# Attention step of a fused transformer layer: two quads' sums in one bank region, projections in even steps and transposes in odd ones

## The chip, the cores and the metric

The kernel runs on one core of a Trainium2 chip. The metric is the device time of the whole kernel in microseconds (us). Engines: PE (TensorE, with PEld for its weight loads), DVE (VectorE), ACT (ScalarE), POOL (GpSimd), SP (SyncE, which issues most DMAs).

## What is computed

Sixteen sequences of 256 tokens with 128 features. The input is normalised (no gain), goes through causal attention with 16 heads of 8 features, and beside it through a mixture of eight expert networks (one shared, seven routed, two of these for each token). The results are added to the input.

```
xn = layernorm(x)
q, k, v = xn @ in_proj.T            # 16 heads of 8, q / sqrt(8)
att = softmax(q @ k.T + causal mask) @ v @ out_proj.T
w = top 2 of softmax(xn @ wr.T + rb), made to sum to 1
ffn = expert(xn; shared) + sum_e w[e] * expert(xn; e)   # expert: (silu(x g) * (x u)) d
out = x + att + ffn
```

## The kernel before

Each engine runs its own list of instructions in order, written out by hand; semaphores (`wait_ge`, `then_inc`) tie the lists together. There are three parts.

*The front*: rounds f = 0 to 15, one for each sequence ("batch"): normalise, transpose the tokens, split them into a high and a low part, values and routing logits. Between some rounds `FRONT` places the first attention steps, with negative numbers. `idle` are matmuls without use that fill PE's pauses (L1023).

*The attention loop*: 64 steps n, `quad(n)` = (batch b, quad j of four heads). A step works on several quads at once. PE's `step(n)` (L984): first scores (`scores(n, 0)`: for the row maxima of quad n+3 and, transposed, for the exponentials of quad n), the transposes of the sums of quad n-2 (L996), the sums of quad n-1 (`sums`, L976 and L979: exponentials times values, into columns 256 to 511 of bank J), second scores, a side job (`side`: query projection at j = 0, key projection at j = 1 for batch b+3, transposes of the scaled sums of batch b-1 at j = 3, two counts for the routing) into columns 256 to 511 of bank X, and `maxima(n+2)` into columns 0 to 255 of J.

ACT's `step(n)` (L690): exponential of one pair of heads (L702), `unscaled(n-2)` (L688: sums out of bank X), exponential of the other pair, the copy for the side job (L711 the high part of a projection, L720 the turned sums), sums from J to `ot` (L732), `queries(n+2)` (L679), and at j = 0 the batch's values into zero-padded columns (L740). POOL's step: a causal select behind each exponential (L616), up to step 22 splitting expert weights (`split_block`), and in steps 23 to 62 altogether 64 indirect DMAs (`send`, L592), between and behind the selects: one in 16 of the 40 steps, two in 24. DVE's `step(n)` (L1334): first row maximum (L1345), a piece of the routing (steps in `N_ROUTE`), second row maximum, the low part of a projection (L1379), the negated maxima (L1358 to L1361), and at j = 2 `scaled(b-1)`: reciprocal (L1325) and multiply (L1329). SP's step loads heads' queries and keys (L485), and stores a batch's projections at j = 2 (L475).

The loop around an exponential: both pairs of heads use the same two banks for their transposed scores, so the second scores of a step wait for the first exponential, and the next step's first scores for the second. Two engines never use one bank at the same time, which is what many of the waits are for (`bank_read`).

*The experts*: `NT * MT` units u of gate, up and down products. Steps 64, 65 and 66 of attention lie in its units 0, 2 and 4.

The printed functions are those that the diff touches.

## Time and profile before

| what | value |
|---|---|
| median of 3 runs | 467.76 us (467.54 to 468.66) |
| profiled execution | 465.75 us, its span 464.0 us |
| PE busy | 431.9 us (93%) |
| DVE busy | 360.9 us (78%) |
| ACT busy | 315.1 us (68%) |
| POOL busy | 295.4 us (64%) |

The profile is one execution. "Busy" is the time in which an engine had an instruction under way; matmuls are pipelined and their ends are modelled. "[x <-E L]" behind an instruction says that its engine was idle for x us ahead of it and what ended that. "issue" is a wait that the profile has no releaser for. In views by time, neighbouring instructions of a kind are one row with their number ("x2"). TensorE's granted clock was full throughout.

### The profile page before, as it was taken

The page shows a single profiled execution, that of the slowest core. Times are in us where ns is not written, and L with a number is a line of the kernel's source. Part 1 is how long each engine was busy: PE and PEld are TensorE (multiplying, and loading weights), DVE is VectorE, ACT ScalarE, POOL GpSimd, SP SyncE. Part 2 cuts the span into 40 slices and gives each one's busy share as a digit, 9 for nine tenths or more (in the row PEclk, how much of TensorE's full clock was granted, in tenths as well). Part 3 has the DMA queues.
Part 4 walks back from the last instruction along what each step waited for, and adds up shares of the span by engine and source line. Part 5 has one row for each costly group of instructions (what it writes and reads, how often), then busy time and mean ns, then how long its engine had stood idle before and what let it go on. Part 6 is the DMA issues. An engine that isn't in the chain of part 4 may idle for free.

```text
span 464.0 us, 12501 instructions
## 1 busy us (share of the span) xinstructions
PE 431.9 (93%) x3983; PEld 323.9 (70%) x3987; DVE 360.9 (78%) x802; ACT 315.1 (68%) x709; POOL 295.4 (64%) x423
## 2 busy tenths in 40 slices
PE   8888898989899999999888999999999999999995
PEld 3766556656666666666666577888888888887783
DVE  5885999999878887877777077777777777776986
ACT  2756777767677777777676866666767776666552
POOL 1425888788888888888888900447457588775200
PEclk9999999999999999999999999999999999999999
DMA  8777799999875666655549226768868867822762
GB/s 232 225 226 256 199 378 292 296 325 353 283 247 159 172 188 173 184 161 153 154 114 335 69 59 181 255 195 279 288 210 279 282 209 258 270 92 68 254 182 70
DMA packets 60415, 99.84 MB, mean 215 GB/s; under 512 B 11045, under 2 KB 29226, under 8 KB 59328
## 3 DMA queue, kind: packets, MB, share of 16 engines
q1 hardware_dynamic: 55872, 90.57, 62.1%
q0 software_dynamic: 4480, 8.47, 5.5%
q8 instruction: 34, 0.56, 0.5%
q14 instruction: 29, 0.24, 0.2%
HBM read 60.85 MB, written 38.94 MB: 215 GB/s over the span
## 4 chain that ended last, share of the span: by engine, by line
PE 62%; DVE 13%; POOL 5%; ACT 4%; issue 3%; SPq 2%; DMA 1%; DVEq 0%; POOLq 0%; ACTq 0%
PE ps L846 12%; PE ps L847 12%; PE ps L848 12%; DVE sb_blockmax L1345 7%; PE ps L915 5%; PE ps L976 5%; PE ps L923 4%; ACT sb_work L702 3%; POOL xs L592 3%; PE ps L1145 3%; POOL sb_work L616 2%; PE ps L996 2%; PE ps L1134 2%; PE ps L979 2%; SPq L475 1%
## 5 line engine op out<-in xcount | busy, mean ns | idle before, releaser
L1345 DVE TENSOR_REDUCE sb_blockmax<-ps 128x6 f32<-128x768 f32 x128 | 121.5, 956 | 30.1 <-PE ps L923 24.4
L702 ACT ACTIVATE sb_work<-ps 128x768 f32<-128x768 f32 x128 | 104.4, 815 | 55.5 <-PE ps L911 54.2
L644 POOL DMA_INDIRECT ys<-sb_v_all,sb_xn_all x76 | 80.0, 1053 | 64.0 <-DVE sb_v_all L1466 46.4
L616 POOL TENSOR_SCALAR_AFFINE_SELECT sb_work<-sb_work 128x512 f32<-128x512 f32 x128 | 82.5, 646 | 24.9 <-ACT sb_work L702 23.2
L847 PE MATMUL ps<-sb_ring,sb_wb 128*128 128x512 f32 (+5 forms) x231 | 83.1, 360 | 0.0
L592 POOL DMA_INDIRECT xs<-sb_xn_all,sb_posu x64 | 62.8, 981 | 10.7 <-issue 10.7
L1444 DVE TENSOR_TENSOR sb_v_all<-ps,sb_v_all 128x512 f32<-128x512 f32 (+3 forms) x93 | 57.3, 616 | 14.1 <-ACT sb_v_all L793 9.9
L915 PE MATMUL ps<-sb_ring 32*128 32x256 f32 x256 | 49.2, 374 | 13.0 <-ACT sb_work L702 7.2
L793 ACT ACTIVATE sb_v_all<-ps 128x512 f32<-128x512 f32 (+3 forms) x93 | 49.8, 535 | 6.2 <-PE ps L848 5.4
L915 PEld LDWEIGHTS ps<-sb_ring 32*128 32x128 f32 x256 | 25.4, 181 | 36.6 <-issue 33.1
L846 PE MATMUL ps<-sb_ring,sb_wb 128*128 128x512 f32 (+1 forms) x138 | 50.8, 368 | 0.0
L923 PE MATMUL ps<-sb_mask_b,sb_ident_b 128*128 128x256 bf16 x256 | 50.2, 278 | 0.0
L907 PE MATMUL ps<-sb_ring 32*128 32x256 f32 x256 | 49.2, 381 | 0.4 <-ACT sb_work L702 0.3
L848 PE MATMUL ps<-sb_ring,sb_wb 128*128 128x512 f32 (+1 forms) x138 | 48.9, 355 | 0.0
L847 PEld LDWEIGHTS ps<-sb_ring,sb_wb 128*128 128x128 f32 (+2 forms) x231 | 42.5, 184 | 6.1
L976 PE MATMUL ps<-sb_work 128*32 128x256 f32 x512 | 40.9, 390 | 4.2 <-issue 1.6
L801 ACT ACTIVATE sb_qk_l<-sb_v_all 128x512 fp32r<-128x512 f32 (+3 forms) x46 | 26.7, 581 | 26.5 <-DVE sb_v_all L1444 20.7
L801 ACT ACTIVATE sb_qk_h<-sb_v_all 128x512 fp32r<-128x512 f32 (+3 forms) x47 | 26.9, 573 | 25.3 <-DVE sb_v_all L1444 19.2
L1452 DVE TENSOR_TENSOR sb_ring<-sb_v_all,sb_qk_h 128x512 fp32r<-128x512 f32 (+3 forms) x47 | 29.8, 633 | 15.8 <-ACT sb_qk_h L801 15.4
L1452 DVE TENSOR_TENSOR sb_ring<-sb_v_all,sb_qk_l 128x512 fp32r<-128x512 f32 (+3 forms) x46 | 29.3, 637 | 12.6 <-ACT sb_qk_l L801 11.7
L586 POOL TENSOR_TENSOR sb_wb<-sb_o_all,sb_wb 128x128 fp32r<-128x128 f32 (+1 forms) x72 | 30.9, 456 | 2.0
L919 PE MATMUL ps<-sb_ring 32*128 32x128 f32 x256 | 30.1, 217 | 0.0
(165 smaller groups left out, 1071.3 us busy)
## 6 DMA issues: line engine op xcount, KB each, us to landing
sb_wb<-wd SPq DMA_DIRECT2D x50, 384.0 KB, 4.3
sb_ring<-qk SPq DMA_DIRECT2D x64, 256.0 KB, 3.4
wd<-sb_wb SPq DMA_DIRECT2D x8, 1088.0 KB, 6.0
sb_wb<-wd SPq DMA_DIRECT2D x25, 320.0 KB, 3.4
xs<-sb_o_all SPq DMA_DIRECT2D x19, 260.0 KB, 3.7
qk<-sb_ring SPq DMA_DIRECT2D x32, 128.0 KB
sb_work<-ys SPq DMA_DIRECT2D x16, 256.0 KB, 3.3
sb_xn_all<-xs SPq DMA_DIRECT2D x15, 260.0 KB, 3.6
```

The source lines that it names most:

```text
L592: pool.indirect_dma_start(out=xs_d, out_offset=bass.IndirectOffsetOnAxis(ap=posu[:, k, t:t + 1], axis=0), in_=xn_all[:, t, :], in_offset=N ...
L616: pool.affine_select(out=o, in_=o, compare_op=ALU.is_ge, fill=0.0, base=0, pattern=[[0, 4], [1, 128]], channel_multiplier=-1)\
L644: pool.indirect_dma_start(out=ys_d, out_offset=bass.IndirectOffsetOnAxis(ap=row, axis=0), in_=yst[i % NYS][:, EMB * j:EMB * j + EMB], in_o ...
L702: act.activation(part.rearrange("p (k h q) -> p h k q", h=2, q=128), ps[:, 4:6, 0:HEAD].rearrange("p h (k q) -> p h k q", q=128), ACT.Exp, ...
L846: pe.matmul(out, wh, xh_, start=start, stop=False, skip_group_check=True)
L847: pe.matmul(out, wh, xl_, start=False, stop=False, skip_group_check=True)
L848: return pe.matmul(out, wl, xh_, start=False, stop=stop, skip_group_check=True)
L915: return pe.matmul(S[h][:, 0:256], q, k, start=True, stop=False, skip_group_check=True)
L923: return pe.matmul(out, ident_b[:, :], mask_b[:, :].unsqueeze(1).to_broadcast([128, 2, 128]), start=False, stop=True, skip_group_check=True)
L976: pe.matmul(J[32 * h:32 * h + 32, 256:512], v_sb[b % 2][:, 0, 4 * j + h, :], p[:, h // 2, h % 2, 1:3, :], start=True, stop=False, skip_gro ...
L1345: dve.tensor_reduce(blockmax[:, a:b + 1, 0:3], ps[:, a:b + 1, 0:HEAD].rearrange("p h (k c) -> p h k c", c=128), AX.X, ALU.max).then_inc(s[ ...
L1452: dve.tensor_tensor(hl[u % 2][0:n, 0:z], hf[u % 2][0:n, 0:z], hh[u % 2][0:n, 0:z].bitcast(F32), ALU.subtract).then_inc(s["hl"], 1)
```

## The change

The values of odd quads are laid 16 columns further right in their 32 zero-padded columns than those of even quads. The sums of an odd quad are added to those of the even one before it, in the same region of bank J (`start` is set for even quads only, and `maxima` sets it for even m only from m = 2 on). So one copy to `ot`, one pair of transposes and one copy out of bank X, now with 144 columns instead of 72, serve two quads.

PE's transposes of sums move from between first scores and sums to the end of odd steps (`across`), together with the turned sums of batch b-2 (at j = 1) and the counts; the projections stand in even steps (`project`: keys of batch b+3 at j = 0, queries of batch b+4 at j = 2). ACT does the copies out of bank X between the two exponentials of the following step (`between`) and copies a batch's values in two halves in odd steps (`batch_values`). DVE does the low part of a projection one step after PE's projection, between the two row maxima and ahead of the routing (`projection_low`), and the multiply of `scaled` in two halves. The front begins at step -14; the keys of batch 2 move from round 7 to round 5, the queries of batch 3 from step 0 to round 9, and the idle matmuls of rounds 10, 12 and 13 wait for `lq` 4. Out of the diff here: counts, buffers' views and waits that only change their numbers.

```diff
 
 
...
+        STEPS = range(-14, NQ + 3)
+
+        FRONT = {0: range(-14, -10), 2: range(-10, -6), 5: [-6, -5, -4], 7: [-3], 9: [-2], 11: [-1]}
         SENDS = TOPK * TILES
 
...
         def isb(b):
             return 0 <= b < NB
 
+        def projected(n):
+
+
+            b, j = quad(n)
+            x = b + 4 if j == 2 else b + 3
+            return (x, j == 0) if j in (0, 2) and isb(x) else None
+
+        def pair_out(n):
+
+            return (n - 3) // 2 if n % 2 and 0 <= (n - 3) // 2 < NQ // 2 else None
+
         def turned(n):
 
 
             b, j = quad(n)
-            return b - 1 if j == 3 and isb(b - 1) and isb(b) else NB - 1 if n == NQ + 2 else None
+            return b - 2 if j == 1 and isb(b - 2) else NB - 1 if n == NQ + 2 else None
 
         def side_out(n):
 
...
+            def unscaled(p):
...
+                c, half = divmod(p, 2)
+                act.wait_ge(s["T"], p + 1)
+                if half == 0 and c >= 2:
                     act.wait_ge(s["nm"], c - 1)
-                view = X[:, 0:256].rearrange("p (t h c) -> p t h c", t=2, c=32)
-                act.activation(xo[c % 2][:, :, j, :, :], view[:, :, :, 0:HD + 1], ACT.Copy).then_inc(s["xc"], 1)
+                view = X[:, 0:256].rearrange("p (t k x) -> p t k x", t=2, k=8)
+                act.activation(xo[c % 2][:, :, half, :, :, :].rearrange("p t h e c -> p t (h e) c"),
+                               view[:, :, :, 0:HD + 1], ACT.Copy)\
+                    .then_inc(s["xc"], 1)
...
+            def projection_high(n):
+
+                x, keys = projected(n)
+                act.wait_ge(s["pk" if keys else "pq"], x + 1)
+                if isb(x - 2):
+                    act.wait_ge(s_qd[(x - 2) % 2], stored(x - 2))
+                at = 256 if keys else 0
+                act.activation(qk_h[x % 2][:, at:at + 256], side_out(n), ACT.Copy)\
+                    .then_inc(s["hk" if keys else "hq"], 1)
...
+            def between(n):
+
+
+                if n % 2:
+                    if projected(n - 1) is not None:
+                        projection_high(n - 1)
+                    return
+                if pair_out(n - 1) is not None:
+                    unscaled(pair_out(n - 1))
+                if turned(n - 1) is not None:
+                    turned_out(turned(n - 1))
...
+            def batch_values(b, e):
+
...
+                part = v_all[:, 2 * b:2 * b + 2, :].rearrange("p s (j e h d) -> p (s j) e h d", j=2, e=2, h=4)
+                act.activation(v_pair[b % 2][:, :, e, :, 16 * e:16 * e + HD], part[:, :, e, :, :], ACT.Copy)\
+                    .then_inc(s["va"], 1)
...
                 if isq(n):
                     for k, pair in enumerate(PAIRS[::-1]):
-                        if k and isq(n - 2):
-                            unscaled(n - 2)
+                        if k:
+                            between(n)
...
-                if isq(n - 1):
+                elif n >= NQ:
+                    between(n)
+                elif projected(n) is not None:
+                    projection_high(n)
+                if n >= 2 and n % 2 == 0 and isq(n - 1):
+                    p = n // 2 - 1
...
+                    if p:
+                        act.wait_ge(s["T"], p)
                     act.activation(ot[:, :], J[:, 256:512], ACT.Copy).then_inc(s["OT"], 1)
...
+                if n == 0:
+                    batch_values(0, 0)
+                    batch_values(0, 1)
+                if isq(n) and j % 2:
+                    batch_values(b + 1, j // 2)
...
+            def project(n):
...
+                x, keys = projected(n)
...
+                elif n > -4:
+                    pe.wait_ge(s["lq" if keys else "lk"], x + 1 if keys else x)
+                    if pair_out(n - 1) is not None:
+                        pe.wait_ge(s["xc"], pair_out(n - 1) + 1)
+                    if turned(n - 1) is not None:
+                        pe.wait_ge(s["oT"], turned(n - 1) + 1)
...
+                pe.wait_ge(s["xl"], x + 1)
+                cols, o = slice(x * SEQ, (x + 1) * SEQ), S_IN + 128 * keys
+                mm3(side_out(n), small_h[:, o:o + 128], small_l[:, o:o + 128], xh_all[:, cols], xl_all[:, cols],
+                    True, True).then_inc(s["pk" if keys else "pq"], 1)
+
+            def across(n):
+
+
+                if projected(n - 1) is not None:
+                    x, keys = projected(n - 1)
+                    pe.wait_ge(s["lk" if keys else "lq"], x + 1)
+                if turned(n - 2) is not None:
+                    pe.wait_ge(s["oT"], turned(n - 2) + 1)
+                if n - 2 in N_COUNT:
...
+                p = pair_out(n)
+                if p:
+                    pe.wait_ge(s["xc"], p)
                 if turned(n) is not None:
...
+                    turn(turned(n))
...
+                if p is not None:
+                    pe.wait_ge(s["OT"], p + 1)
+                    for t in range(2):
+                        last = pe.transpose(X[:, 128 * t:128 * t + 128], ot[:, 128 * t:128 * t + 128], ident)
+                    last.then_inc(s["T"], 1)
+
+            def turn(c):
+                pe.wait_ge(s["nm"], c + 1)
+                for t in range(2):
+                    last = pe.transpose(X[:, 256 + 128 * t:384 + 128 * t], on[c % 2][:, t, :], ident)
+                last.then_inc(s["tT"], 1)
...
                     pe.matmul(J[:, 128 * t:128 * t + 128], mexp[m % 3][:, 1 - t, :], ident_r[:, :],
-                              start=(t == 0), stop=False, skip_group_check=True)
+                              start=(t == 0 and (m < 2 or m % 2 == 0)), stop=False, skip_group_check=True)
...
+                pe.wait_ge(s["va"], 2 * b + 2)
+                if n >= 2 and n % 2 == 0:
+                    pe.wait_ge(s["OT"], n // 2)
 
                 p = P[n % 2].rearrange("p (a k h q) -> p a h k q", a=2, h=2, q=128)
                 for h in range(4):
                     pe.matmul(J[32 * h:32 * h + 32, 256:512], v_sb[b % 2][:, 0, 4 * j + h, :],
-                              p[:, h // 2, h % 2, 1:3, :], start=True, stop=False, skip_group_check=True)
+                              p[:, h // 2, h % 2, 1:3, :], start=(n % 2 == 0), stop=False, skip_group_check=True)
...
-                if isq(n - 2):
-                    bank_read(n - 1)
-                    pe.wait_ge(s["OT"], n - 1)
-                    if isq(n - 3):
-                        pe.wait_ge(s["xc"], n - 2)
-                    for t in range(2):
-                        last = pe.transpose(X[:, 128 * t:128 * t + 128], ot[:, 128 * t:128 * t + 128], ident)
-                    last.then_inc(s["T"], 1)
                 if isq(n - 1):
                     sums(n - 1)
                 if isq(n) or isq(n + 3):
                     scores(n, 1)
-                if n > -4:
-                    bank_read(n - 1)
-                if isq(n - 2) and has_side(n):
-                    pe.wait_ge(s["xc"], n - 1)
-                side(n)
+                if projected(n) is not None:
+                    project(n)
                 if n >= 0 and isq(n + 2):
                     maxima(n + 2)
+                if 0 < n < NQ + 2 and n % 2:
+                    across(n)
+                if n == NQ + 2:
+                    pe.wait_ge(s["oT"], NB - 1)
+                    turn(NB - 1)
...
                 if f < NB - 2 and (f < 5 or f not in FRONT):
                     if f > 5:
-                        pe.wait_ge(s["lq"], 3)
-                    if f > 7:
                         pe.wait_ge(s["lk"], 3)
+                    if f > 9:
+                        pe.wait_ge(s["lq"], 4)
                     idle(1 if f in FRONT else 3)
...
-                sums = xo[c % 2][:, :, :, :, :].rearrange("p t j h c -> p (t j h) c")
+                sums = xo[c % 2][:, :, :, :, :, :].rearrange("p t i h e c -> p (t i h e) c")
                 dve.reciprocal(rden[:, :], sums[:, :, HD]).then_inc(s["rc"], 1)
                 dve.wait_ge(s["rc"], c + 1)
                 if c >= 2:
                     dve.wait_ge(s["tT"], c - 1)
-                dve.tensor_tensor(on[c % 2][:, :, :].rearrange("p t (j d) -> p (t j) d", d=HD), sums[:, :, 0:HD],
-                                  rden[:, :].unsqueeze(2).to_broadcast([128, 32, HD]), ALU.mult).then_inc(s["nm"], 1)
+                out = on[c % 2][:, :, :].rearrange("p t (i e h d) -> p (t i) e h d", i=2, e=2, h=4)
+                parts = xo[c % 2][:, :, :, :, :, :].rearrange("p t i h e c -> p (t i) h e c")
+                shares = rden[:, :].rearrange("p (g h e) -> p g h e", h=4, e=2)
+                for e in range(2):
+                    last = dve.tensor_tensor(out[:, :, e, :, :], parts[:, :, :, e, 0:HD],
+                                             shares[:, :, :, e].unsqueeze(3).to_broadcast([128, 4, 4, HD]), ALU.mult)
+                last.then_inc(s["nm"], 1)
...
                 if isq(m):
                     maximum(0)
                 if n == NQ + 1:
                     scaled(NB - 1)
+                if n > 0 and n % 2 and projected(n - 1) is not None:
+                    projection_low(n - 1)
                 if n in N_ROUTE:
                     next(route)
                 if isq(m):
                     maximum(1)
                     if n < 0:
                         negative()
-                if j in (0, 1) and isb(b + 3):
-                    dve.wait_ge(s["hk" if j else "hq"], b + 4)
-                    if isb(b + 1):
-                        dve.wait_ge(s_qd[(b + 1) % 2], stored(b + 1))
-                    part = slice(256 * j, 256 * j + 256)
-                    dve.tensor_tensor(qk_l[(b + 3) % 2][:, part], side_out(n), qk_h[(b + 3) % 2][:, part].bitcast(F32),
-                                      ALU.subtract).then_inc(s["lk" if j else "lq"], 1)
+                if n < 0 and projected(n) is not None:
+                    projection_low(n)
                 if isq(m) and n >= 0:
                     negative()
```

## Rows read from the trace of the kernel before

**Rows 1.** The attention loop's two stretches: busy us of each engine with its instructions.

```profile
46.10:123.00 76.90, 68.49 (x926) 46.57 (x928) 71.33 (x168) 56.19 (x132) 64.05 (x129) 1.00 0.93 306
...
123.00:263.00 140.00, 129.12 (x1744) 89.32 (x1744) 104.52 (x240) 104.09 (x245) 119.00 (x155) 1.00 0.61 179
```

**Rows 2.** The chain of waits: shares by line from 76 to 122 us, and one piece.

```profile
by line: DVE sb_blockmax L1345 53.5%; issue 7.8%; DVE sb_mexp L1361 3.9%; DVE sb_mexp L1358 3.2%; DVE ps L1359 2.4%; DVE sb_rden L1325 2.4%; DVE sb_rt_buf L1276 2.3%; DVE sb_r_s L1214 2.1%; DVE sb_rt_buf L1263 1.9%; DVE sb_qk_l L1379 1.9%; 
...
122.22 0.30 DVE sb_qk_l L1379
```

**Rows 3.** Who waited for whom on DVE, 46 to 123 us: total, times, longest.

```profile
DVE sb_blockmax L1345 <- PE ps L923: 1.0, 2, 0.5
```

**Rows 4.** POOL in order of time: start us, us, instruction, idle before it.

```profile
125.10 0.63 POOL L616 TENSOR_SCALAR_AFFINE_SELECT sb_work<-sb_work 128x512 f32<-128x512 f32 x1 [0.38 <-ACT sb_work L702]
...
221.24 0.65 POOL L616 TENSOR_SCALAR_AFFINE_SELECT sb_work<-sb_work 128x512 f32<-128x512 f32 x1
222.06 0.97 POOL L592 DMA_INDIRECT xs<-sb_xn_all,sb_posu  x1 [0.17 <-issue]
223.05 0.64 POOL L616 TENSOR_SCALAR_AFFINE_SELECT sb_work<-sb_work 128x512 f32<-128x512 f32 x1
...
259.93 0.64 POOL L616 TENSOR_SCALAR_AFFINE_SELECT sb_work<-sb_work 128x512 f32<-128x512 f32 x1
```

**Rows 5.** One step with one send, all engines in order of time.

```profile
182.45 0.39 ACT L732 ACTIVATE sb_ot<-ps 128x256 f32<-128x256 f32 x1
...
182.97 0.84 ACT L702 ACTIVATE sb_work<-ps 128x768 f32<-128x768 f32 x1
...
183.53 0.64 PE L976 MATMUL ps<-sb_work 128*32 128x256 f32 x8
...
184.31 0.38 PE L915 MATMUL ps<-sb_ring 32*128 32x256 f32 x2
...
184.81 0.81 ACT L702 ACTIVATE sb_work<-ps 128x768 f32<-128x768 f32 x1 [0.87 <-PE ps L911]
...
185.69 0.63 POOL L616 TENSOR_SCALAR_AFFINE_SELECT sb_work<-sb_work 128x512 f32<-128x512 f32 x1 [0.46 <-ACT sb_work L702]
```

**Rows 6.** The transposes of sums: groups of instructions by shape.

```profile
L996 PE MATMUL ps<-sb_const,sb_ot 128*128 128x128 f32 x128 | 25.9, 284 | 2.2 <-DVE sb_ring L1379 1.3 <-DVE sb_qk_l L1379 0.8
```

**Rows 7.** DVE in order of time, steps 1, 2 and 9.

```profile
50.13 0.96 DVE L1345 TENSOR_REDUCE sb_blockmax<-ps 128x6 f32<-128x768 f32 x1
...
51.01 0.42 DVE L1379 TENSOR_TENSOR sb_ring<-ps,sb_ring 128x256 fp32r<-128x256 f32 x1
...
51.90 0.96 DVE L1345 TENSOR_REDUCE sb_blockmax<-ps 128x6 f32<-128x768 f32 x1
...
53.74 0.95 DVE L1345 TENSOR_REDUCE sb_blockmax<-ps 128x6 f32<-128x768 f32 x1
...
55.36 0.96 DVE L1345 TENSOR_REDUCE sb_blockmax<-ps 128x6 f32<-128x768 f32 x1
...
76.14 0.96 DVE L1345 TENSOR_REDUCE sb_blockmax<-ps 128x6 f32<-128x768 f32 x1 [0.54 <-PE ps L923]
```

**Rows 8.** The multiply that scales: ns min/median/max, first and last start us.

```profile
L1329 DVE TENSOR_TENSOR sb_on<-sb_xo,sb_rden x16: 424/425/687, 68.9 to 269.7; 128x256 f32<-128x256 f32 x16
```

**Rows 9.** The front's rounds 10 and 11, in order of time.

```profile
33.11 0.59 PE L1026 MATMUL ps<-sb_busy 128*128 128x512 bf16 x2
...
33.74 0.17 DVE L1361 TENSOR_TENSOR sb_mexp<-ps,sb_mexp 128x8 fp32r<-128x8 f32 x1
33.82 0.41 DVE L1400 TENSOR_TENSOR sb_xl_all<-ps,sb_xh_all 128x256 fp32r<-128x256 f32 x1
...
34.29 0.33 PE L857 MATMUL ps<-sb_small_h,sb_xh_all 128*128 128x136 f32 x1 [0.58 <-DVE sb_xl_all L1400]
```

**Rows 10.** The way into the experts, in order of time.

```profile
263.27 1.28 ACT L656 ACT_TABLE_LOAD   x1
...
267.51 0.47 PE L846 MATMUL ps<-sb_qk_h,sb_wb 128*128 128x512 f32 x1 [0.35 <-DVE sb_ring L1452]
```

124 lines of the change are left out of this document (47 added, 77 removed).

## The prediction

> **What bounds the kernel now.** The first view is the busy time by stretch [rows 1]. The attention loop's steps 0 to 63 run from 46.1 us (the second half of step 0) to about 263 us; before them lies a front, behind them the experts. PE is busy in both stretches of attention (68.5 of 76.9 us, 129.1 of 140.0 us), so the page invites the reading "TensorE is the bound, and a transpose saved is time saved". The rows beside it speak against that: in the first stretch of attention DVE has 71.3 of 76.9 us, in the second POOL has 119.0 of 140.0 us. So I read what releases whom.
>
> 46 to 123 us (steps 0 to 22). The chain of waits goes through DVE, over half of it through the row maxima [rows 2], and DVE waited for PE only twice, 1.0 us in all [rows 3]. The rest of its 5.6 idle us is the short pause before each instruction that needs its predecessor's result. DVE is the bound here: two maxima of 0.96 us in each step, the routing, and the low parts of the projections. PE, ACT and POOL are followers.
>
> 123 to 263 us (steps 23 to 62). POOL issues 64 indirect DMAs, none before: the code spreads them as one in 16 steps and two in 24. Between two selects with a send between them the distance is 1.81 us (221.24 to 223.05 [rows 4]), so a step with two sends costs 3.61 us from its last select to the next, whatever PE does. A step with one send costs POOL less, and then a loop through four engines decides: sums start to scores 0.78, scores to exponential 0.50, exponential to select 0.88, select 0.63, and, estimated from the hand-over between exponential (ends 185.62) and select (185.69), 0.1 to the next sums: together 2.89 us [rows 5]. No transpose is in that loop. Lower bound of the stretch: 24 x 3.61 + 16 x 2.89 = 132.9 us. Measured, from the end of the select at 125.10 (125.73) to the end of that at 259.93 (260.57): 134.84 us [rows 4]. Only 1.9 us are left for anything done to PE, ACT or DVE.
>
> **The change part by part.** The sum is made against the profiled execution: 465.75 us, span 464.0 us, 2.01 us below the median of 467.76 us.
>
> *Transposes, copies, copies out halved on PE and ACT.* 64 of 128 transposes go; all took 25.9 us of PE [rows 6], so 13 us go, and 32 copies of 0.38 us on ACT [rows 5] with 32 copies out. From 46 to 123 us this buys what DVE waits for, at most 1.0 us. One of the two waits (0.54 us before 76.14 us [rows 7], behind a load by SP that starts when PE's step 5 is done) I expect to vanish: without its transposes PE reaches that release some 0.3 us earlier, and DVE arrives later by its own extra work. From 123 to 263 us it buys at most the 1.9 us above. About 0.5 us of these lie at steps 29 and 30, where a routing step puts DVE on the chain; that stays. Another 0.4 us I give back: with the transposes gone ACT's chain of copy, query copy and exponential (182.45 to 182.97 us, and 0.84 us behind it [rows 5]) has to fit between scores and scores, and the larger copy out and the turned copy now both stand between two exponentials. Taken: -1.0 us. Ends: -1.9 and, if the added waits bite in every one of the 16 short steps with 0.1 us more than the slack, +0.6 us.
>
> *Low parts of projections moved on DVE.* Until now the low part stands behind the second maximum, where it covers the pause before the negated maxima. With it, second maximum to next first one is 50.13 to 51.90 = 1.77 us; without it 53.74 to 55.36 = 1.62 us [rows 7]. So it costs 0.15 us where it is, although it takes 0.41 us, 0.33 us of it beyond the overlap of 0.08 us with the maximum ahead of it (50.13 + 0.96 against 51.01). The change puts it between the two maxima, where nothing is covered: 0.33 us. Steps 0 to 8: four new at 0.33 against five old at 0.15, +0.57 us; steps 9 to 22: seven against seven, +1.26 us. All are on the bound engine. If the new place covered a pause too, the price is 0: bounds 0 and +1.8 us; I take the upper one, since the two steps compared are the same but for that instruction. (What waits behind it on DVE is the routing and the second maximum.) It needs ACT's high part, issued between the exponentials; the scores that the second exponential waits for need the first exponential too, so I let it be there in time.
>
> *Scaling split in two multiplies.* One of 256 columns takes 425 ns [rows 8]; an 8-column one took 0.17 us [rows 9]; on that line a 128-column one is 0.30 us, two less an overlap of 0.08 us are 0.51 us: +0.09 us for each batch, four batches before step 22, +0.4 us. Bounds: 0 and, if each of the two is stretched as the longest was (687 ns against 425 ns), 4 x 0.6 = 2.4 us. The median is the nearest row. The stretched ones ran beside POOL. The Trainium skill (SBUF — State Buffer, section "SBUF: two separate sides") says that a DVE instruction with two SBUF inputs and a GpSimd instruction that reads SBUF exclude one another for a whole instruction. By that each added multiply could stand behind a whole select. The trace agrees only in part: the worst of 16 lost 0.26 us, the mean 0.05 us.
>
> So the DVE stretch: 0.57 + 1.26 + 0.4 - 0.54 = +1.7 us at step 21; the other wait, before the first exponential's scores, stays. In before, step 22 then lost time since the transposes waited for the low part at 122.22 us [rows 2]; without them its second scores hang on the negated maxima alone, which returns about 0.6 us. Taken: +1.1 us, ends -0.6 (the prices above at zero) and +3.5.
>
> *The front.* Seven projections stand in front of the loop instead of six, the queries of batch 3 newly at round 9. The idle matmuls of round 10 now wait for their low part. They started at 33.11 us, and the values behind them at 34.29 us, when the low tokens (33.82 us) were there [rows 9]. The new low part comes in before these, behind the negated maxima that end at 33.91 us: it ends at 34.24 us, the idle matmuls start at 34.3 us and take 0.6 us (two of the three took 0.59), and the values start at 34.9 us. What follows on PE up to the first exponential hangs on that: +0.6 us. Ends: 0 (an idle matmul is off the path and later rounds have slack) and +0.9. The second key projection, moved from round 7 to round 5, costs ACT a copy of 0.38 us there and gives DVE and ACT the same back two rounds on: 0.
>
> *Values in two halves, memsets, the SP queue.* Two halves lie in odd steps, where ACT no longer copies sums: 0 here. The cover is ACT's wait ahead of the second exponential (0.87 us before 184.81 us [rows 5]); with it gone each costs at most a copy, 0.38 us. POOL's two added memsets of small columns lie in the front where it idles. SP's loads and stores keep their order, and the low parts they wait for come a maximum (0.96 us) earlier in the step; the queue waits for PE's scores otherwise. 0.
>
> *The end.* ACT's last table load starts at 263.27 us [rows 10], behind a copy of turned sums and one of sums; both leave step 63, and two copies stand 0.52 us from start to start [rows 5], so it starts 0.5 us earlier. The first expert product then lacks its 0.35 us wait at 267.51 us; one pair of transposes of scaled sums moves into the experts' stretch, one pair of sums leaves it. Taken -0.4 us, ends -0.6 and +0.2.
>
> Sum: 0.6 (front) + 1.1 (DVE stretch) - 1.0 (POOL stretch) - 0.4 (end) = +0.3 us; 465.75 + 0.3 = 466.05, and with 2.01 us to the median 468.1 us.
>
> **The rivals.** First, *PE is the bound after all*: its 93% are right and the 13 us come off: 455 us. Against it: two selects 1.81 us apart with a send between, 48 times, and DVE without a gap. 3%.
>
> Second, *the two costs on DVE are covered*: the low part in its new place covers a pause, the front has slack, and the POOL stretch gives its whole 1.9 us: -0.3 - 1.9 - 0.5 = -2.7 us, 465.0 us. For it: the 1.9 us are there, and each cost is some tenths. 19%; between it and the forecast the time is 466 to 467 us.
>
> Third, the other side: *DVE waits for ACT in the odd steps*. The low part stands ahead of the routing and the second maximum. If ACT's high part (exponential 0.81, then copy 0.38 us) ends later than the first maximum, the bound engine stands still, and the second maximum, the negated ones and PE's next scores behind it. It decides as soon as the first maximum of a step starts within 0.2 us of the first exponential. Price: up to 0.3 us in each of 11 steps, +3.3 us on the sum: 471.4 us; half the steps: 469.7 us. For it: where DVE has caught up with PE, as at 76.14 us [rows 7], first scores and first maximum are together; against it: it had caught up only twice [rows 3]. 22%. The lock between DVE and POOL as a whole select (0.64 us) for each added multiply would be 4 x 0.64, less the 0.4 counted: +2.2 us, 470.3 us; 3%.
>
> Fourth, *nothing is shared in effect*: the new wait of the projection for the copy out of the same bank delays PE as much as the transposes did. Then the POOL stretch stays, since POOL has slack for neither: 469.1 us. 3%.
>
> **How the numbers follow.** Forecast 50%, around 468.1 us (466.4 to 469.4 by its own ends); first rival 3%, second 19%, third 25% with the lock, fourth 3%. A measurement tells 0.3%, 1.4 us, from no change: bounds 466.36 and 469.16 us. Faster: the first rival, most of the second and a little of the forecast: 0.21. Slower: most of the third, half of the fourth, some of the forecast: 0.28. Same: 0.51. The range reaches into the second and third: 465.8 to 470.4 us.
>
> **What would show it.** From the last select of step 22 to that of step 62: 133.8 us (right: 132.9 to 134.5). Two-send steps still 3.61 us. DVE from 46 to 123 us: no longer wait for PE than before, low part between two maxima, end of the stretch later by 1 to 2 us. Idle matmuls of round 10 at 34.3 us, values behind them at 34.9 us. PE's idle time in attention grows by about the 13 us of transposes. Wrong would be the whole reading if two-send steps got shorter; the DVE part, if the low part's start leaves a gap after the first maximum (third rival) or if second-to-first maximum falls by more than 0.15 us (second).

## The result and the profile after

The changed kernel takes 468.91 us (median of 18 runs, 467.90 to 473.63), the kernel before on the same chip 466.87 us (18 runs): ratio 1.0059, 95% interval 1.0036 to 1.0082. It is slower by 2 to 3 us (1.7 to 3.8 us by the interval). The profiled run of the changed kernel has a span of 467.8 us at a mean granted clock of 0.982, that of before 464.0 us at 0.998 (half only in its last 2.0 us, behind all of PE's work), which was a quick run of its kernel (465.75 us, 1.1 us below the 18 runs' median). So the 3.8 us between the two profiles overstate the difference; their stretches show where it lies.

I cut both spans where POOL's last select of a step ends (us; the last column is the time at half granted clock within steps 1 to 22):

```
                     step 0 ends  steps 1-22  steps 23-62  rest     half clock in 1-22
before               47.28        78.45       134.83       203.43   0
changed              47.60        83.65       133.56       202.98   13.7
difference           +0.32        +5.20       -1.27        -0.45
predicted            +0.6         +1.1        -1.0         -0.4
```

Three of four terms hold. The fourth, the stretch that DVE bounds, is off by 4 us. First the same two stretches as in [rows 1], of the changed kernel: span, then busy us of PE, its weight loads, DVE, ACT and POOL, the granted clock, DMA share, GB/s.

```profile
46.10:123.00 76.90, 65.34 (x834) 42.75 (x832) 68.11 (x158) 48.91 (x106) 59.63 (x121) 0.91 0.86 286
123.00:263.00 140.00, 124.97 (x1743) 85.48 (x1739) 111.27 (x263) 101.46 (x216) 119.60 (x158) 1.00 0.61 189
```

In the first, PE is busy for 3.2 us less, although 13.7 us at half clock lengthen its matmuls. DVE, the bound before with 71.3 us, is now busy for 68.1 us only (by 123 us the changed kernel has done about a step less), and the granted clock is 0.91 for 1.00. DVE's waits for PE from 46 to 131 us (total us, times, longest), first in the kernel before, then in the changed one ([rows 3] has those of before up to 123 us):

```profile
DVE sb_blockmax L1345 <- PE ps L923: 2.1, 4, 0.6
```

```profile
DVE sb_blockmax L1406 <- PE ps L983: 3.8, 7, 1.0
```

and, in the same stretch, PE's waits for DVE in the changed kernel, first those of its first scores for the negated maxima, then those for the low part:

```profile
PE ps L975 <- DVE sb_mexp L1422: 5.1, 8, 1.0
PE ps L953 <- DVE sb_qk_l L1431: 1.4, 2, 1.1
PE ps L953 <- DVE sb_ring L1431: 1.3, 1, 1.3
PE ps L947 <- DVE sb_ring L1431: 1.3, 1, 1.3
PE ps L947 <- DVE sb_qk_l L1431: 0.9, 1, 0.9
```

The first row is PE following the engine that bounds it. The others are new in size (1.8 us in before, the longest 0.8). L953 is the pair of transposes at the end of odd steps, L947 the counting matmul that stands there in steps 7 and 11, L1431 the low part. Four of PE's five waits for the low part lie at the end of steps 7, 11, 15 and 19, before 73.17, 87.67, 102.94 and 119.87 us. This is the third, at the end of step 15, on DVE in order of time:

```profile
98.55 0.96 DVE L1406 TENSOR_REDUCE sb_blockmax<-ps 128x6 f32<-128x768 f32 x1
99.96 0.17 DVE L1419 TENSOR_REDUCE sb_mexp<-sb_blockmax 128x8 fp32r<-128x16 f32 x1 [0.45 <-DVE sb_blockmax L1406]
...
100.33 0.35 DVE L1381 RECIPROCAL sb_rden<-sb_xo 128x32 f32<-128x32 f32 x1
100.71 0.97 DVE L1389 TENSOR_TENSOR sb_on<-sb_xo,sb_rden 128x128 f32<-128x128 f32 x2
101.61 0.94 DVE L1406 TENSOR_REDUCE sb_blockmax<-ps 128x6 f32<-128x768 f32 x1
102.47 0.41 DVE L1431 TENSOR_TENSOR sb_ring<-ps,sb_ring 128x256 fp32r<-128x256 f32 x1
```

and on PE:

```profile
101.30 0.33 PE L1023 MATMUL ps<-sb_ring,sb_ident_r 128*128 128x256 f32 x1
102.94 0.68 PE L953 MATMUL ps<-sb_const,sb_ot 128*128 128x128 f32 x2 [1.30 <-DVE sb_ring L1431]
103.54 0.58 PE L975 MATMUL ps<-sb_ring 32*128 32x256 f32 x2
...
104.71 1.08 PE L1038 MATMUL ps<-sb_work 128*32 128x256 f32 x8
```

DVE comes out of step 14, which has a routing piece, the reciprocal and both multiplies (0.97 us, for 0.43 to 0.64 us before). It begins the first maximum of step 15 at 101.61 and the low part at 102.47, without a gap: DVE does not wait for ACT. PE has had nothing to do since 101.63 and stands 1.30 us, with the next scores queued behind the transposes. From 103.0 us on its matmuls are long: scores 0.58 us where they take 0.38 [rows 5], sums 1.08 us for 0.64. The windows around it, columns as above:

```profile
99.00:103.00 4.00, 2.33 (x32) 1.35 (x32) 3.48 (x10) 2.55 (x7) 3.54 (x8) 1.00 0.87 262
103.00:109.80 6.80, 6.80 (x58) 4.17 (x61) 4.48 (x11) 2.85 (x6) 4.04 (x9) 0.50 0.94 335
...
116.00:120.10 4.10, 2.02 (x31) 1.36 (x23) 3.94 (x10) 2.01 (x5) 3.22 (x7) 0.99 0.82 272
120.10:123.50 3.40, 3.40 (x36) 1.74 (x34) 3.01 (x7) 0.99 (x2) 1.93 (x4) 0.51 0.80 266
```

In the stretches ahead of these two falls PE was busy for 2.33 of 4.00 and 2.02 of 4.10 us; behind them the granted clock is at the lower of its two levels (1.2 of 2.4 GHz), and PE is busy without a pause: for these 6.8 and 3.4 us PE is the bound, and DVE has gaps (4.48 of 6.80 us). Some steps as time between the last selects (h: some of it at half clock; the other kernels are described below):

```
step   before   changed   changed, second chip   late_scale   both
8      3.16     4.73      4.74                   3.73         3.73
12     4.17     4.72      5.61 h                 4.17         4.17
16     3.90     5.88 h    4.51                   3.90         3.90
17     3.47     4.16 h    3.06                   3.07         3.22
20     3.93     5.57 h    5.09 h                 3.90         3.90
```

A step that is longer is not all loss, since its neighbours can be shorter: step 9 takes 3.32 us in the changed kernel and 3.97 us in before, and in late_scale steps 10, 14, 18 and 22 take 4.46, 4.08, 4.68 and 4.03 us, for 3.68, 3.75, 3.70 and 3.44 us in before. What DVE itself spends is in the part on the prediction.

### The profile page after: what moved, and what is told of

It reads as the page before. It is cut to its first block, busy times and chain, and to the rows that moved or that the text cites. A ratio compares the mean times of both kernels' runs of the same rounds, so it can differ in the third digit from the quotient of the medians.

```text
span 467.8 us, 12331 instructions
## 1 busy us (share of the span) xinstructions
PE 428.4 (92%) x3919; PEld 318.7 (68%) x3923; DVE 365.2 (78%) x818; ACT 307.7 (66%) x661; POOL 295.5 (63%) x425
## 4 chain that ended last, share of the span: by engine, by line
PE 49%; POOL 2%; issue 1%; ACT 1%; DVE 1%; DVEq 0%
PE ps L892 12%; PE ps L893 12%; PE ps L894 12%; PE ps L1201 2%; PE ps L1038 2%; PE ps L975 2%; PE ps L1190 2%; PE ps L983 1%; ACT sb_work L765 1%; POOL xs L607 1%; PE ps L1041 1%; POOL sb_work L631 1%; PE ps L953 0%; PE ps L979 0%; PE ps L1021 0%
## 5 line engine op out<-in xcount | busy, mean ns | idle before, releaser
L631 POOL TENSOR_SCALAR_AFFINE_SELECT sb_work<-sb_work 128x512 f32<-128x512 f32 x128 | 82.3, 644 | 29.4 <-ACT sb_work L765 27.7
L1511 DVE TENSOR_TENSOR sb_v_all<-ps,sb_v_all 128x512 f32<-128x512 f32 (+3 forms) x93 | 57.3, 616 | 10.1 <-ACT sb_v_all L839 5.7
L975 PE MATMUL ps<-sb_ring 32*128 32x256 f32 x256 | 50.3, 384 | 9.7 <-DVE sb_mexp L1422 5.1
L1038 PE MATMUL ps<-sb_work 128*32 128x256 f32 x512 | 42.3, 401 | 12.4 <-issue 6.4
L983 PE MATMUL ps<-sb_mask_b,sb_ident_b 128*128 128x256 bf16 x256 | 51.3, 283 | 0.0
L967 PE MATMUL ps<-sb_ring 32*128 32x256 f32 x256 | 50.3, 390 | 0.4 <-ACT sb_work L765 0.3
L1519 DVE TENSOR_TENSOR sb_ring<-sb_v_all,sb_qk_l 128x512 fp32r<-128x512 f32 (+3 forms) x46 | 29.6, 643 | 13.1 <-ACT sb_qk_l L847 12.2
L1038 PEld LDWEIGHTS ps<-sb_work 128*32 128x32 f32 x512 | 11.1, 109 | 28.3 <-issue 15.1
```

Of the source, the lines that this page charges most:

```text
L631: pool.affine_select(out=o, in_=o, compare_op=ALU.is_ge, fill=0.0, base=0, pattern=[[0, 4], [1, 128]], channel_multiplier=-1)\
L975: return pe.matmul(S[h][:, 0:256], q, k, start=True, stop=False, skip_group_check=True)
L1038: pe.matmul(J[32 * h:32 * h + 32, 256:512], v_sb[b % 2][:, 0, 4 * j + h, :], p[:, h // 2, h % 2, 1:3, :], start=(n % 2 == 0), stop=False, ...
L1511: dve.tensor_tensor(hf[u % 2][0:n, 0:z], ub(u)[0:n, 0:z], s_b[u % 2][0:n, 0:z], ALU.mult).then_inc(s["mul"], 1)
L1519: dve.tensor_tensor(hl[u % 2][0:n, 0:z], hf[u % 2][0:n, 0:z], hh[u % 2][0:n, 0:z].bitcast(F32), ALU.subtract).then_inc(s["hl"], 1)
```

## The experiments

The kernels ran on two other chips. Each has its ratio to the kernel before on its own chip, so ratios can be set side by side, times only within a chip. Theory: PE's new wait for the low part, and what the granted clock does behind it, make the loss. Rivals: the split multiply; the alternation as such; the clock alone.

**changed_again**: the changed kernel as it is.

> The changed kernel as it is, beside the experiments on the same chip. Measured once at 1.0059 of the kernel before (1.0036 to 1.0082). Clock theory (PE, thinned by 64 transposes and standing at waits for the low part, drops to half its clock for some us of steps 3 to 20, which the DVE-bound stretch then feels): ratio 1.003 to 1.008, and executions with a lower mean granted clock are longer. DVE theory (only the low parts at 0.33 us and the split multiply cost): about the same ratio, +1.1 us less than nothing elsewhere, and no tie between clock and time.

Measured: 489.83 us for 483.89 us, 1.0126 (1.0076 to 1.0176). The loss is there on a second chip, larger than either theory expected (1.003 to 1.008), and so are PE's five waits for the low part (the longest 1.3, 1.3, 1.1 and 0.9 us).

**before_again**: the kernel before, a profile only.

> The kernel before as it is, for its profile on the chip of these experiments: steps 0 to 22 in about 78.5 us on a chip like the first, 22 to 62 in 134.8 us. Clock theory as first put (only the change thins PE enough): granted clock whole up to the end. If the kernel before also shows stretches at half clock in steps 0 to 22, the clock is no property of the change.

Measured: 487.51 us in the profiled run. On this chip the kernel before has falls of the clock too, 3.4 us in steps 1 to 22 and 10.2 us up to 481 us. Ahead of the first PE was busy 2.27 of 4.30 us:

```profile
105.00:109.30 4.30, 2.27 (x39) 1.68 (x30) 3.15 (x8) 1.98 (x6) 3.69 (x8) 1.00 1.02 378
109.30:112.70 3.40, 3.40 (x35) 1.98 (x32) 1.65 (x3) 1.33 (x3) 0.64 (x1) 0.50 1.00 336
```

In this stretch PE waited 2.0 us, not for DVE but for a load of queries and keys:

```profile
108.88 0.38 PE L915 MATMUL ps<-sb_ring 32*128 32x256 f32 x2 [2.03 <-DMA sb_ring<-qk]
```

So the fall is no property of the change. In the changed kernel it is more frequent: the mean clock of the six runs of changed_again is 0.978, that of 23 runs of before beside them 0.991. Over the 18 runs of the changed kernel on the first chip, the mean granted clock ranges from 0.990 (four runs, 467.9 to 468.6 us) to 0.975 and 0.968 (the two slowest runs, 472.95 and 473.63 us).

**double**: the changed kernel, the pair of transposes done twice.

```diff
-                    for t in range(2):
+                    for t in (0, 1, 0, 1):
                         last = pe.transpose(X[:, 128 * t:128 * t + 128], ot[:, 128 * t:128 * t + 128], ident)
```

> Each pair of transposes of sums is done twice, into the same place: PE has all the work back that the change took, waits unchanged. Clock theory: the granted clock stays whole, the stretch of steps 0 to 22 falls from 83.6 us to about 80 us, the total to 0 to +1 us of the kernel before (ratio 0.999 to 1.003). DVE theory: PE work more or less changes nothing there, ratio as the changed kernel's or up to 0.5 us above it. If PE were a bound: +12 us.

Measured: 1.0104 (1.0067 to 1.0141), as the changed kernel within the intervals. The first clock theory had the clock whole here; in the profile 13.7 us of steps 1 to 22 are at half clock, so it is refuted. Putting the 64 transposes back costs nothing that can be told: PE's amount of work is not the bound, and the loss has not to do with their number.

**thin**: the opposite, on the kernel before: of each pair of transposes the first is left out up to step 24 (that part of the sums is stale).

```diff
-                    for t in range(2):
+                    for t in (range(2) if n > 24 else range(1, 2)):
```

> The kernel before, with the first of each pair of transposes of sums left out up to step 24 (the left half of the sums is then stale: part of the output is not computed). PE loses there what the change takes from it, and no wait, order or DVE work is changed. If thinning alone lets the clock fall: granted clock below whole in steps 0 to 22, total +0.5 to +3 us. If it is the new wait: clock whole, total 0 to -0.5 us, since PE is not the bound. DVE theory: the same 0 to -0.5 us.

Measured: 0.9986 (0.9952 to 1.0020). Less work on PE alone gives nothing and costs nothing. Its profile caught 13.7 us at half clock (108.2 to 121.9 us) behind a stretch with PE busy 2.37 of 4.20 us, and here too PE's wait was one of 2.0 us for a load. Over its 12 runs the mean clock is 0.991, within 0.001 of that of before. One profile shows how the clock falls, not how often; the frequency is in the runs.

**split**: the kernel before, only its multiply in two halves.

```diff
-                dve.tensor_tensor(on[c % 2][:, :, :].rearrange("p t (j d) -> p (t j) d", d=HD), sums[:, :, 0:HD],
-                                  rden[:, :].unsqueeze(2).to_broadcast([128, 32, HD]), ALU.mult).then_inc(s["nm"], 1)
+                for e in range(2):
+                    last = dve.tensor_tensor(on[c % 2][:, e, :].rearrange("p (j d) -> p j d", d=HD),
+                                             sums[:, 16 * e:16 * e + 16, 0:HD],
+                                             rden[:, 16 * e:16 * e + 16].unsqueeze(2).to_broadcast([128, 16, HD]),
+                                             ALU.mult)
+                last.then_inc(s["nm"], 1)
```

> The kernel before with the multiply of the scaling in two halves, nothing else. By my term: +0.09 us for each of 5 batches in steps 0 to 22, +0.4 us, ratio 0.999 to 1.002. By the lock between DVE and POOL (each half can wait for a POOL instruction): +0.45 us for each, +2 us, ratio 1.003 to 1.006, and rows of the halves above 0.6 us for two.

Measured: 1.0039 (1.0009 to 1.0068), about 1.9 us. From 46 to 131 us its ten halves take 4.78 us (4.40 us from start to end of each pair, since the two overlap), the five whole multiplies of before on that chip 2.51 us. The difference, 1.9 us, is of the size of the loss, but the interval is wide, and the profiled run also has a wait of PE of 2.1 us for a load at 75.96 us with 3.4 us of half clock behind it, which is not the multiply's. The line of the halves in split, ns min/median/max:

```profile
L1330 DVE TENSOR_TENSOR sb_on<-sb_xo,sb_rden x32: 276/292/722, 68.3 to 275.3; 128x128 f32<-128x128 f32 x32
```

and in the changed kernel:

```profile
L1389 DVE TENSOR_TENSOR sb_on<-sb_xo,sb_rden x32: 276/291/755, 71.0 to 273.7; 128x128 f32<-128x128 f32 x32
```

The medians are near what the prediction took, the halves in the stretch that DVE bounds are not. The changed kernel's first pair, with its longest half, on DVE:

```profile
70.96 0.95 DVE L1389 TENSOR_TENSOR sb_on<-sb_xo,sb_rden 128x128 f32<-128x128 f32 x2
```

and POOL at the same time:

```profile
70.93 0.64 POOL L631 TENSOR_SCALAR_AFFINE_SELECT sb_work<-sb_work 128x512 f32<-128x512 f32 x1
```

The first half starts 0.03 us behind the select and ends 0.14 us after it. The same at 100.97 us: select 100.85 to 101.54, half ends 101.69. The eight kernels with halves have 256 of them. 25 had no POOL instruction beside them and took 276 to 293 ns. All 89 that took longer than 300 ns had one, but so had 142 that stayed under 300 ns. What POOL does makes the difference: of the 89, 76 had a select or a piece of the weights' splitting beside them, of the 142 all but 5 an indirect DMA (15 of them with the last 0.12 us of a select).

**next_step**: the changed kernel with the transposes and the waits ahead of them moved from the end of the odd step into the next, between its first scores and its sums.

```diff
+                if 0 < n - 1 < NQ and n % 2 == 0:
+                    across(n - 1)
                 if isq(n - 1):
                     sums(n - 1)
...
-                if 0 < n < NQ + 2 and n % 2:
+                if n == NQ + 1:
                     across(n)
```

> The transposes of a pair stand where they stood before the change, between first scores and sums, one step later than in the changed kernel; everything else as changed. PE then does not stand at the end of odd steps for DVE's low part (1.30 us at 102.94 us in the trace). Clock theory with that wait as the cause of PE's idling: dips fewer or gone, stretch of steps 0 to 22 down by 2 to 4 us, ratio 0.998 to 1.002. If thinning alone lets the clock fall: dips stay, ratio 1.003 to 1.008. DVE theory: no change to the ratio.

Measured: 1.0064 (1.0029 to 1.0099) for 1.0126: better, though the intervals overlap (1.0076 to 1.0176 for the changed kernel). No wait of PE for the low part is left from 46 to 131 us. I had expected fewer falls of the clock or none. The profiled run, one of the slower ones (491.47 us), has three in steps 1 to 22, 13.7 us in all, which take 84.39 us, and the ratio lies above my 0.998 to 1.002, where I had put the case that less work on PE alone lets the clock fall. thin does not bear that case out. So the wait may be a part of the loss, but it is not the only thing behind which the clock falls. The rest is of the size of split.

**low_back**: the changed kernel with the low part again behind the second maximum, the transposes still at the end of the odd step.

```diff
-                if n > 0 and n % 2 and projected(n - 1) is not None:
-                    projection_low(n - 1)
                 if n in N_ROUTE:
                     next(route)
                 if isq(m):
                     maximum(1)
                     if n < 0:
                         negative()
+                if n > 0 and n % 2 and projected(n - 1) is not None:
+                    projection_low(n - 1)
```

> The changed kernel with the low part of a projection put back behind the second maximum of its odd step (DVE), PE's order as changed, so the transposes at the end of odd steps wait for it still longer. DVE theory (0.18 us more for each of 11 low parts): DVE's stretch 2 us shorter, ratio 1.001 to 1.003. Wait theory (what costs is PE standing at the end of odd steps for the low part): stretch not shorter or longer by up to 3 us, ratio 1.005 to 1.013.

Measured: 1.0679 (1.0616 to 1.0741), steps 1 to 22 take 101.3 us, mean granted clock 0.941. The profiled run was the slowest of its six (521.27 us), with 37.5 us of steps 1 to 22 at half clock. PE's largest waits from 46 to 131 us:

```profile
PE ps L953 <- DVE sb_ring L1431: 3.2, 1, 3.2
PE ps L953 <- DVE sb_qk_l L1431: 2.5, 2, 1.3
PE ps L947 <- DVE sb_ring L1431: 2.4, 1, 2.4
```

Here the low part comes one maximum and one routing piece later, and PE has to stand for it at the end of every odd step that has one. The instruction that I had priced at 0.15 us here and 0.33 us there makes the stretch 19 us longer (101.3 for 82.3 us in changed_again) in the place that I had called cheaper, much of it at half clock: what counts is not its own time on DVE but who waits for it. The place between the maxima was needed.

**next_low**: both edits together: low part behind the second maximum, transposes in the next step.

> Both undone: low part behind the second maximum, transposes of a pair between first scores and sums of the next step. Left of the change: pairs, projections in even steps, copies between exponentials, split multiply, longer front. If low part's place and the wait at the end of odd steps are the cause together: steps 0 to 22 in 79 to 80 us (by the first chip), 22 to 62 in 133.5 us, ratio 0.996 to 1.000. If the split multiply or something else of the change is the cause: 1.003 or more.

Measured: 1.0247 (1.0199 to 1.0296). I had expected 0.996 to 1.000: a clear miss. The later transposes do not outrun the later low part. PE waits for it 8.1 us from 46 to 131 us, and its waits of 1.1 us and more (60.94, 77.04, 94.74, 111.90 and 128.68 us) are each followed by half clock:

```profile
91.00:95.00 4.00, 1.98 (x26) 1.36 (x26) 3.86 (x10) 2.10 (x4) 3.83 (x9) 1.00 0.86 272
95.00:98.40 3.40, 3.40 (x33) 2.06 (x31) 1.27 (x3) 1.33 (x3) 0.24 (x1) 0.50 0.96 367
```

22 us of its steps 1 to 22 are at half clock. Of the 15 steps there that have none, 14 have none in before_again either: they take 3.43 us on average, for 3.54 us there. But the steps left out are those with the long waits, so this shows only that the rest of the work is not dearer.

**The last group** (a third chip) asks what makes the low part late at just those four steps, and tests both causes. Steps 6, 10, 14 and 18 have a routing piece and the scaling of a block on DVE; steps 8, 12, 16 and 20 have no routing piece. The turned transposes need the scaled block only in step 9, 13, 17, 21. The changed kernel itself was not run on this chip.

**late_scale**: the changed kernel, scaling two steps later.

```diff
-                if j == 2 and 1 <= b < NB:
-                    scaled(b - 1)
+                if j == 0 and 2 <= b <= NB:
+                    scaled(b - 2)
```

> The changed kernel; only the reciprocal and the multiply of a block move on VectorE, from the end of steps 6, 10, 14, 18 to the end of steps 8, 12, 16, 20, whose VectorE has no piece of the routing (in all 64 steps alike, two steps later). Theory A: steps 6, 10, 14 and 18 load VectorE with a routing piece, the reciprocal and the multiply, so in steps 7, 11, 15 and 19 its low part comes late and TensorE, at the end of the step, stands 0.9 to 1.3 us for it; in the profiles of the changed kernel half granted clock follows in the next step, which then takes 4.9 us against 3.6. With the move these waits for the low part fall under 0.5 us, the stretch from step 0 to step 22 takes 79.5 to 81.5 us (changed kernel on this slower chip 82.25, kernel before 80.93), and the ratio falls from 1.013 to 1.002 to 1.006. Theory B (the split multiply alone is the cost, wherever it stands): the ratio stays at 1.004 or above, with the waits gone. Theory C (the cost is the alternation of projection and transposes itself, whose waits for the low part come back somewhere else): ratio 1.008 to 1.013, stretch 82 us or more.

**one_mult**: the changed kernel, the multiply whole again.

```diff
-                for e in range(2):
-                    last = dve.tensor_tensor(out[:, :, e, :, :], parts[:, :, :, e, 0:HD],
-                                             shares[:, :, :, e].unsqueeze(3).to_broadcast([128, 4, 4, HD]), ALU.mult)
-                last.then_inc(s["nm"], 1)
+                dve.tensor_tensor(on[c % 2][:, :, :].rearrange("p t (g d) -> p (t g) d", d=HD), sums[:, :, 0:HD],
+                                  rden[:, :].unsqueeze(2).to_broadcast([128, 32, HD]), ALU.mult).then_inc(s["nm"], 1)
...
-                            f["attn_out_proj_weight"].T], axis=1)
+                            f["attn_out_proj_weight"].T.reshape(2, 2, 4, HD, EMB).transpose(0, 2, 1, 3, 4)
+                            .reshape(EMB, EMB)], axis=1)
```

> The changed kernel, with the multiply of a block in one instruction again: the block stays in the order in which the copy leaves it (second quad's heads beside the first's), and the rows of the output projection's weight are stored in that order, so nothing else changes. Theory B: the halves took 3.7 to 4.6 us in the stretch of 46 to 131 us, for a whole multiply of 2.5 to 2.6 us in the kernel before; the same split in the kernel before cost 1.0039. So VectorE gets back 1.2 to 2.0 us, all of it in the stretch that it bounds, and the ratio falls by 0.003 to 0.004, to 1.008 to 1.010, with the instruction at 0.43 to 0.64 us. Theory A (only the waits at the end of steps 7, 11, 15 and 19 matter): these get shorter by the same 0.3 us each, so the ratio may fall by more, to 1.005. If the halves cost nothing on the path, the ratio stays at 1.012 to 1.013.

**both**: the two together.

> The two edits together on the changed kernel: multiply in one instruction, and reciprocal and multiply two steps later. Theories A and B together: the stretch from step 0 to step 22 takes 78.5 to 80.5 us, no wait of TensorE for the low part over 0.5 us, stretch from step 22 to 62 as in the other changed kernels, ratio 0.996 to 1.001: the gain forecast for the POOL-bound stretch and the end then comes through. Theory C (the alternation itself costs): 1.004 to 1.009.

**both_next**: the two, and the move of next_step.

> As the last, and the pair of transposes and the waits ahead of it also move from the end of the odd step to the next step, between its first scores and its sums. That move alone brought the changed kernel from 1.0126 to 1.0064. Theory A: it removed the same waits as the later multiply does, so with them gone it brings nothing more: within 0.003 of the last kernel, 0.995 to 1.001. If the two remove different waits, it is better than the last by 0.003 to 0.006.

Measured, all beside 481.67 us of before on that chip:

```
             us       ratio (95%)                 steps 1-22 of the profile   half clock in it   mean clock of 12 runs
late_scale   484.12   1.0041 (1.0005 to 1.0077)   80.37                       0                  0.991
one_mult     485.44   1.0061 (1.0030 to 1.0091)   84.37                       about 12           0.984
both         481.72   0.9988 (0.9954 to 1.0023)   79.46                       3.4                0.989
both_next    483.35   1.0001 (0.9959 to 1.0042)   81.74                       13.7               0.987
```

The ratio of late_scale lands in its range (1.002 to 1.006), where that of the split multiply alone (1.004 or above, with the waits gone) begins too; that of both lies inside its own. The end of step 15 in late_scale, on DVE:

```profile
99.93 0.96 DVE L1406 TENSOR_REDUCE sb_blockmax<-ps 128x6 f32<-128x768 f32 x1
100.80 0.41 DVE L1431 TENSOR_TENSOR sb_ring<-ps,sb_ring 128x256 fp32r<-128x256 f32 x1
```

and on PE:

```profile
101.27 0.44 PE L953 MATMUL ps<-sb_const,sb_ot 128*128 128x128 f32 x2 [0.23 <-DVE sb_ring L1431]
```

The wait of 1.30 us is 0.23 us, and DVE waits for PE nowhere longer than 0.12 us in steps 1 to 21. One part of the expectation is missed: there are waits over 0.5 us, in a new place. The turned transposes (L959) of steps 9, 13, 17 and 21 now wait 0.7 us at the longest, since the scaling stands in the step ahead. Their rows among PE's waits from 46 to 131 us:

```profile
PE ps L959 <- DVE sb_qk_l L1431: 1.4, 2, 0.7
PE ps L959 <- DVE sb_ring L1431: 1.3, 2, 0.7
```

With the whole multiply too (both) they are 0.4 us at the longest.

one_mult came out a little better than the split alone explains (1.0061 where 1.008 to 1.010 was expected for it). But its whole multiplies did not take the 0.43 to 0.64 us expected: four in steps 6 to 18 took 0.88, 0.91, 0.67 and 0.43 us, 0.5 us less in all than the four pairs of the changed kernel. The two longest start with a select; the first of them and, on POOL, that select:

```profile
70.58 0.88 DVE L1385 TENSOR_TENSOR sb_on<-sb_xo,sb_rden 128x256 f32<-128x256 f32 x1
```

```profile
70.55 0.64 POOL L631 TENSOR_SCALAR_AFFINE_SELECT sb_work<-sb_work 128x512 f32<-128x512 f32 x1
```

So the stretch comes from where the multiply falls beside POOL; a whole one is not spared. In both the four take 2.4 us, for 3.7 us of the four pairs in late_scale.

both is level with the kernel before (no measurable gain over it) and, on the same chip, 2.4 us below late_scale and 3.7 us below one_mult. So each edit brings something beside the other. Against one_mult the intervals are apart; against late_scale they overlap, so there the gain is likely and not certain. The clock goes with the late scaling: its mean is 0.991 and 0.989 with it, 0.984 in one_mult. both_next is level with both, as expected of two moves that remove the same waits, and its 13.7 us at half clock (56.9 to 70.5 us) stand without any wait for the low part.

## Why the prediction was right and wrong

The time is inside the range (465.8 to 470.4 us), 0.8 us above the 468.1 us forecast. The call "same" was wrong: the kernel is slower by 0.6%, on the side given 0.28, and the change is 2 to 3 us where +0.3 us was forecast. That the time came so near is luck: the forecast had the profiled run 3.5 us too short and its distance to the median 2.6 us too large, and the two errors cancel but for 0.8 us. By the steps of the prediction:

- *What bounds what*: right. Two-send steps still take 3.6 us, steps 23 to 62 take 133.56 us (133.8 predicted, bound 132.9). PE's work is not the bound while the clock is whole (double, thin). PE's transposes at L953 take 13.1 us for 25.9 [rows 6], and the time grew. PE's idle time grew by 3.15 and 4.15 us in the two stretches of [rows 1], 7.3 us, and not by about 13: in the first the half clock lengthens the matmuls that are left.
- *The front*: +0.32 us at the end of step 0, predicted +0.6. The idle matmuls start at 34.31 us as predicted (34.3), but the values behind them at 34.55, not 34.9: I had added the idle matmuls' whole 0.6 us. Against 34.29 [rows 9] that is +0.26 us.

```profile
34.31 0.59 PE L1082 MATMUL ps<-sb_busy 128*128 128x512 bf16 x2
...
34.55 0.41 PE L903 MATMUL ps<-sb_small_h,sb_xh_all 128*128 128x136 f32 x1
```

- *The end*: -0.45 us, predicted -0.4. The table load starts 2.16 us behind the last select of step 62 (264.81 to 266.97), for 2.70 us before.
- *Low part between the maxima*: its own time there is as costed, 0.33 us (101.61 + 0.94 against 102.47, then 0.41), and it never waited for ACT. So the third rival, DVE standing for ACT's high part, is refuted as a mechanism, though its change (+1.9 to +3.6 us on 467.76 us) would have fitted the result better than the forecast's.
- *The step that failed* is first the sentence in brackets, "what waits behind it on DVE is the routing and the second maximum". It names who stands behind the low part on DVE, and not who waits for it elsewhere: PE, whose transposes of odd steps write the bank that the low part reads. I had such a wait in hand, at 122.22 us [rows 2], and took only the gain of losing it. In before it came to 2.1 us over all 128 transposes [rows 6]. In the changed kernel low part and transposes meet at the end of the odd step, and wherever DVE is a microsecond late (routing and scaling in the step ahead), PE stands. The sum had DVE's waits for PE fall by 0.54 us, gave back another 0.6 us at step 22 and counted nothing for a lower clock; measured, they grew by 2.8 us (next point).
- *What DVE spent*: from its first row maximum of step 1 to that of step 22 (47.92 to 122.98 us in before, 48.09 to 129.18 us in the changed kernel), with its waits for PE over 0.2 us, the rest, and the time at half clock in it:

```
               whole    waits for PE   rest     half clock
before         75.06    0.54           74.52    0
changed        81.10    3.36           77.74    13.7
before_again   77.55    4.00           73.54    3.4
changed_again  79.55    1.20           78.35    6.8
late_scale     77.88    0              77.88    0
one_mult       80.30    3.08           77.22    10.8
both           76.96    0.55           76.40    3.4
```

  The first chip's +6.0 us are +2.8 us of waits for PE and +3.2 us that DVE needs itself. Of the six waits of 3.36 us, 3.1 us lie in a stretch at half clock or up to 1.2 us behind it, the two longest here:

```profile
107.42 0.96 DVE L1406 TENSOR_REDUCE sb_blockmax<-ps 128x6 f32<-128x768 f32 x1 [1.01 <-PE ps L983]
...
109.86 0.96 DVE L1406 TENSOR_REDUCE sb_blockmax<-ps 128x6 f32<-128x768 f32 x1 [0.93 <-PE ps L983]
```

  Behind PE's waits of 1.28 and 0.95 us at 73.17 and 87.67 us the clock stayed whole, and DVE stood for 0.25 us in all (78.14 us). So a wait of PE of about a microsecond cost the bound engine next to nothing by its length; what it cost came with the clock. Longer ones do reach DVE: in low_back, with waits of PE of up to 3.2 us, DVE's waits come to 26.8 us, 6.6 us of them away from any half clock. The 3.2 us are the split multiply, +1.35 us, and the cover that the low part no longer gives ahead of the negated maxima, +2.3 us over 11 of them (0.21 us each, costed at 0.18), less some tenths in the routing.
- *The size at the selects*: of the +5.20 us, an estimate by the step table: steps 4, 16, 17 and 20 take 4.03, 5.88, 4.16 and 5.57 us with half clock, and without it, in profiles of the second chip, 3.75 and 4.51 and 3.06 (changed_again) and 4.85 us (double): 3.5 us are the clock. 1.7 us are left for what I had costed at 1.1. The values without half clock come from another chip and other runs, so this is rough.
- *The multiply*: predicted +0.09 for each block, measured 0.96, 0.62, 0.97 and 0.81 us from start to end of the four pairs up to step 22, for 0.47, 0.64, 0.43 and 0.47 us before: +0.34 us on average, +1.35 us in all, where 0.4 was counted and 2.4 was the bound. The row of before that spoke for it was there, the maximum of 0.69 us in [rows 8]; I took the median of 16, of which eleven lie behind 131 us, ten of them at 424 to 426 ns; the five ahead of that, which count here, took 426 to 637 ns. The Trainium skill (SBUF — State Buffer, section "SBUF: two separate sides") says that such a DVE instruction and a GpSimd instruction reading SBUF exclude one another for a whole instruction. The trace agrees here more than I allowed: a half begun 0.03 us behind a select of 0.64 us took 0.76 us, and split measured 1.9 us for it. Indirect DMAs of POOL mostly left the halves as they were (137 of 150), selects and splits did not.
- *How the whole comes out*: of the 3.8 us between the profiles 2.0 us are left between the 18-run medians (2.8 us by the ratio). The profiled run of before had a clock of 0.998, which 3 of its 74 runs on the other two chips reach; I took its distance to the median (2.01 us) to be the same for both kernels. For the changed one it was -0.6 us: its profiled run of 469.53 us is slower than its median. Part of that distance is the clock, which falls more often in the changed kernel (mean 0.983 over its 18 runs).

What stays open: what makes the clock fall more often. Many falls in the changed kernel, double, low_back and next_low and none in late_scale speak for PE's waits for the low part, but next_step and both_next have falls of 13.7 us without such waits, and the kernel before has them on the second chip behind waits for loads. How the loss of about 1% on the second chip divides between clock, waits and DVE's own work stays open with it.

Nor is it shown that the gain in steps 23 to 62 exists elsewhere. On the second chip it does not: 137.99 us in before_again, 137.91 in next_step, 137.89 in double, and 140.83 us in changed_again, of which 6.8 us are at half clock. On the third, both has 140.49 us with the same 6.8 us, late_scale 137.11 us, and before has no profile. The steps with one send take 3.15 us on the second chip, for 2.90 us, and the whole loop through the four engines is slower there. In before_again POOL waits longer for the exponential, and ACT for the scores, than in [rows 5]; why is not known:

```profile
147.95 0.64 POOL L616 TENSOR_SCALAR_AFFINE_SELECT sb_work<-sb_work 128x512 f32<-128x512 f32 x1 [0.72 <-ACT sb_work L702]
```

```profile
147.07 0.81 ACT L702 ACTIVATE sb_work<-ps 128x768 f32<-128x768 f32 x1 [1.05 <-PE ps L911]
```
